# Three of four adjacency blocks transposed by DMA instead of TensorE, with the loads, stores and degree sums around them moved

## The chip, the core and the metric

One core of a Trainium2 chip runs the whole program. The metric is the device time of one execution in microseconds (us), as a median of several runs; lower is better. Engines are named as in the profile: PE is TensorE (PEld its weight loads), DVE is VectorE, ACT is ScalarE, POOL is GpSimd, SP is SyncE. SPq is the queue from which SP issues DMAs.

## The reference

A graph of 2048 nodes with 256 features; `adj` is a 2048x2048 int32 matrix. Two layers, each behind a layer norm and with a residual:

```python
h = relu(layernorm(x))
mask = (adj > 0)
agg = mask @ h / max(mask.sum(1), 1)
x = x + relu(concat(h @ W_self + b_self, agg @ W_nb + b_nb) @ W_comb + b_comb)

state = relu(layernorm(x))
for _ in range(5):
    a_in  = adj   @ (state @ in_W.T  + in_b)
    a_out = adj.T @ (state @ out_W.T + out_b)
    a = concat(a_in, a_out, state)
    r, z = sigmoid(a @ r_W.T + r_b), sigmoid(a @ z_W.T + z_b)
    h_hat = tanh(concat(a_in, a_out, r * state) @ h_W.T + h_b)
    state = (1 - z) * state + z * h_hat
x = x + tanh(state @ o1_W.T + o1_b) @ o2_W.T + o2_b
```

The second layer needs the adjacency both as it is and transposed, and its row sums and column sums (the "degrees", with which the biases in_b and out_b are multiplied).

## The kernel before

The instruction streams are written out by hand for each engine; semaphores alone order them, so each engine works strictly in the order of its own stream. Nodes go in four blocks of 512 (index b, NB = 4), each of four tiles of 128 rows (BT = 4); there are NT = 16 tiles.

**Loading.** The adjacency comes as 32 pieces of 256 rows x 512 columns, 512 KB of int32 each, into a ring of three slots (`ring`, in the tensor WG). SP issues piece k once ACT has converted piece k-3 (L262 to L266). ACT converts each piece in two instructions to fp16 in `A` (function `convert`, L773) with the row sum as a by-product in `degA`; each conversion adds one to the semaphore `conv`.

**The first layer's loop** (L473 on PE, L855 on ACT, L1111 on DVE) has 64 steps i, with b = i // 16 and m = i % 16. For each step PE transposes four 128x128 fp16 blocks of `A` into a PSUM bank (`turn_adj`, L402; it runs LEAD = 3 steps ahead). The even results are copied to `AT` by ACT, the odd ones by DVE (`move_adj`, L785 and L1047), each copy with the column sum as a by-product in `degT`. DVE makes the mask `AT > 0` (`make_mask`, L1055, four buffers in the tensor DR). PE multiplies (`mean_sum`, L418): four matmuls of 512 columns on `hi_lo` (the normed input, split into two fp16 halves) and four of one column that count the mask's ones. After each block there are two calls of `dense` (L441), the weights of the layer, then on DVE the residual, the next layer norm (`residual`, `row_stats`, `variance`, `newton`, `normed`) and the turned state (`turn_h2`). The result x1 goes from SBUF (`xs`) to DRAM (`x1_d`), issued by POOL (L340), and comes back at the end. ACT copies the finished state to `SN` when that store has landed.

**The spread** (L487 on PE). Before any gate, both products of adjacency and state are made for four blocks: `spread(b)` has 16 tiles of 8 matmuls on `AT`, `A` and `SN`. Blocks 0 and 2 write banks 0 to 3, blocks 1 and 3 banks 4 to 7 (`gate_bank`). ACT and DVE empty the banks (`out_pq`). Two calls of `spread_degrees` (L506) inside spread(0) spread the row sums (w = 0) and column sums (w = 1) over all partitions, 16 matmuls each on diagonal matrices that DVE makes (`diag`, L1153); DVE copies the results out of banks 4 to 7 (`out_degrees`, L1158). Meanwhile SP stores twelve quadrants of `AT` and `A`, 1 MB each, to DRAM (`quad_d`, L274), DVE makes sums of quadrants in place (`quad_sums`, L1203, four instructions for each of x = 0, 1) and SP stores these as well.

**The steps** (L721) then alternate groups of gate matmuls (`gate_group`) with products of stored quadrants (`products`), by a seven-multiplication scheme for 2x2 blocks; n counts halves of the node range from FIRST = -2.

Several things share memory. The normed input `h32` lies in AT[:, 1], the weights' sums `scaled` in AT[:, 2], the fused weights `fusedS` in AT[:, 3]; each must have been used up before `AT` is written there.

## Time and profile before

| what | us |
|---|---|
| runs | 1234.11 median of 3 (1233.86 to 1236.0) |
| profiled execution, its own time | 1233.81 |
| its span | 1232.0 |
| first layer's loop on PE, first mask matmul to the last `dense` of block 3's first half | 27.76 to 139.79 |
| spread(0) to spread(3) | 139.79 to 256.41 |
| from the first gate group on | 256.41 to 1232.0 |

The profiled execution is 0.30 us below the median. All times inside it count from the span's start. A matmul's duration in the rows is longer than the distance to the next, since matmuls are pipelined; the cost of a group of them on PE is read from start to start.

### The profile page before, as it was taken

How to read it: one execution, taken by the hardware profiler on the slowest of the kernel's cores; microseconds unless marked ns; L12 is line 12 of the kernel's file. 1: busy time of each engine (PE TensorE's matmuls, PEld its weight loads, DVE VectorE, ACT ScalarE, POOL GpSimd, SP SyncE). 2: the span in 40 equal slices, each digit the busy share in tenths (PEclk: the TensorE clock that was granted, in tenths of full speed). 3: DMA queues.
4: the chain of work that ended last, by engine and by line, in shares of the span. 5: the costliest groups of instructions: out<-in, count | busy, mean ns of one | idle time of the engine just before them, and what ended most of it. 6: DMA issues, size and time to landing. Idle time of an engine off the chain costs nothing.

```text
span 1232.0 us, 12870 instructions
## 1 busy us (share of the span) xinstructions
PE 1221.4 (99%) x4872; PEld 590.6 (48%) x4872; DVE 759.4 (62%) x1276; ACT 285.0 (23%) x556; POOL 15.4 (1%) x15
## 2 busy tenths in 40 slices
PE   8999999999999999999999999999999999999998
PEld 5666654444444444444444444444444444444445
DVE  6677744787985464487357339726825864662674
ACT  5756200022322021033112113301202230120121
POOL 4000000000000000000000000000000000000000
PEclk9999999999999999999999999999999999999999
DMA  9454643960008604800740660192085039015202
GB/s 330 159 166 172 241 186 126 351 248 0 1 34 317 229 1 159 302 18 34 284 160 0 228 250 1 39 357 82 1 299 179 1 132 332 14 66 207 90 1 69
DMA packets 44507, 180.61 MB, mean 147 GB/s; under 512 B 3490, under 2 KB 13475, under 8 KB 29347
## 3 DMA queue, kind: packets, MB, share of 16 engines
q1 hardware_dynamic: 43440, 176.04, 39.5%
q0 software_dynamic: 720, 3.67, 0.8%
q8 instruction: 36, 0.59, 0.2%
q10 hardware_dynamic: 290, 0.14, 0.0%
q14 instruction: 21, 0.16, 0.0%
HBM read 144.71 MB, written 35.13 MB: 146 GB/s over the span
## 4 chain that ended last, share of the span: by engine, by line
PE 86%; DVE 3%; issue 1%; ACT 0%; DVEq 0%
PE bank L347 84%; PE bank L517 1%; DVE LF L1199 0%; DVE GR L1346 0%; DVE first_GZ L1346 0%; DVE first_GH L1319 0%; DVE first_GZ L1349 0%; DVE GR L1349 0%; DVE ST L1322 0%; DVE u_buf L1383 0%; DVE GR L1303 0%; PE bank L467 0%; ACT GR L951 0%; DVE H L1095 0%; DVE AT L1052 0%
## 5 line engine op out<-in xcount | busy, mean ns | idle before, releaser
L347 PE MATMUL bank<-slot,LF 128*128 128x512 f16 x1792 | 389.4, 379 | 0.0
L347 PEld LDWEIGHTS bank<-slot,LF 128*128 128x128 f16 x1792 | 175.3, 98 | 210.1 <-issue 2.3
L347 PE MATMUL bank<-X,W 128*128 128x512 f32 x384 | 180.5, 592 | 0.0
L347 PE MATMUL bank<-XT,W 128*128 128x512 f32 x288 | 135.3, 592 | 0.0
L347 PEld LDWEIGHTS bank<-X,W 128*128 128x128 f32 x384 | 72.5, 190 | 88.0 <-issue 86.9
L347 PE MATMUL bank<-AT,SN 128*128 (+1 forms) x256 | 97.0, 379 | 0.0
L347 PE MATMUL bank<-A,SN 128*128 (+1 forms) x256 | 97.0, 379 | 0.0
L1245 DVE TENSOR_TENSOR u_buf<-bank,m_buf 128x512 f32<-128x512 f32 x16 | 11.1, 691 | 134.0 <-PE bank L347 134.0
L347 PEld LDWEIGHTS bank<-XT,W 128*128 128x128 f32 x288 | 54.7, 190 | 68.9 <-issue 68.2
L767 ACT ACTIVATE m_buf<-bank 128x512 f32<-128x512 f32 x46 | 27.4, 595 | 231.9 <-PE bank L347 231.9
L347 PE MATMUL bank<-DR,work 128*128 128x512 f16 x256 | 67.1, 386 | 1.8 <-DVE DR L1063 1.6
L347 PE MATMUL bank<-XS,W 128*128 128x512 f32 x128 | 65.4, 592 | 0.0
L347 PE MATMUL bank<-ST,W 128*128 128x512 f32 x120 | 61.3, 592 | 0.0
L951 ACT ACTIVATE GR<-GR,col 128x512 f32<-128x512 f32 x40 | 28.8, 720 | 99.7 <-DVE GR L1349 51.7
L347 PE MATMUL bank<-first_X,W 128*128 128x512 f32 x96 | 45.2, 593 | 0.2 <-DVE RT L1283 0.2
L951 ACT ACTIVATE GZ<-GZ,col 128x512 f32<-128x512 f32 x32 | 23.1, 722 | 85.6 <-DVE GZ L1349 55.3
L951 ACT ACTIVATE GH<-GH,col 128x512 f32<-128x512 f32 x32 | 23.1, 722 | 85.5 <-DVE GH L1349 56.4
L347 PE MATMUL bank<-GR,W 128*128 128x512 f32 x80 | 40.9, 592 | 0.0
L767 ACT ACTIVATE A<-WG 128x512 f16<-128x512 int32 x64 | 39.5, 621 | 0.6 <-DMA WG<-in_adj 0.6
L347 PEld LDWEIGHTS bank<-A,SN 128*128 (+1 forms) x256 | 25.1, 98 | 29.9
L347 PEld LDWEIGHTS bank<-AT,SN 128*128 (+1 forms) x256 | 25.1, 98 | 29.7
L347 PEld LDWEIGHTS bank<-XS,W 128*128 128x128 f32 x128 | 24.3, 190 | 30.6 <-issue 30.6
(217 smaller groups left out, 1420.5 us busy)
## 6 DMA issues: line engine op xcount, KB each, us to landing
slot<-quad_d SPq DMA_DIRECT2D x112, 1024.0 KB, 5.1
WG<-in_adj SPq DMA_DIRECT2D x32, 512.0 KB, 4.2
quad_d<-AT SPq DMA_DIRECT2D x12, 1024.0 KB, 5.0
quad_d<-A SPq DMA_DIRECT2D x12, 1024.0 KB, 8.6
quad_d<-spare SPq DMA_DIRECT2D x4, 1024.0 KB, 4.0
SN<-in_x SPq DMA_DIRECT2D x2, 1024.0 KB, 10.4
x_d<-SN POOLq DMA_DIRECT2D x4, 512.0 KB, 3.2
x1o<-x_d SPq DMA_DIRECT2D x1, 2048.0 KB, 8.4
```

What stands on the lines that cost most here:

```text
L347: return pe.matmul(o, l, r, start=start, stop=stop, skip_group_check=again)
L517: last = pe.transpose(o[:, q * P:q * P + P], ST[:, f, n0:n0 + P], ident)
L767: return nc.scalar.activation(o, i, ACT.Copy, scale=scale, **kw)
L951: nc.scalar.activation(buf[:, tile, :], buf[:, tile, :], ACT.Tanh if j == 2 else ACT.Sigmoid, bias=col[:, 10 + 2 * j + f:11 + 2 * j + f]). ...
L1245: v.tensor_tensor(u3, b[:, :], m1, ALU.add).then_inc(prod_dve, 1)
```

## The change

- Blocks 1 to 3 of `AT` are no longer made by PE, ACT and DVE. SP issues for each of the 12 groups j of four tiles (b = 1 + j // 4, c = j % 4) four DMA transposes from `A` to `AT`, each of 128 partitions x 512 fp16 (128 KB, four 128x128 blocks). A group is issued when `conv` has reached 4(j + 5) and, from the fifth on, when group j - 4 has landed. Block 0 stays as it was.
- `make_mask` of blocks 1 to 3 waits, at each fourth step, for the four transposes of its group.
- The row loads from the fourth piece on are issued by POOL instead of SP. The x1 stores are issued by ACT instead of POOL, ahead of the square root of the layer norm. The store of the fused weights goes from POOL to SP, ahead of the transposes.
- ACT's conversions run further ahead: at step i the count reaches 5 + i + max(0, i - 8) // 3 instead of 5 + i.
- The column sums of blocks 1 to 3, 48 instructions (`column_sums`), are made by ACT behind the loop from `AT`, with a throw-away output in `trash`. DVE's reduction of them, the second set of diagonals, `spread_degrees(1)` and `out_degrees(1)` move from spread(0) into spread(2) and its surroundings, and DVE's `out_degrees(1)` goes between `quad_sums(0, 0)` and `quad_sums(0, 1)`.
- `h32` moves from AT[:, 1] to AT[:, 3], `fusedS` from AT[:, 3] to AT[:, 1].

```diff
 LEAD = 3
+TURNS = 4
...
+        trash = [at(f"trash{i}", (202 + i) * KB, [P, BN], FP16)[:, :] for i in range(2)]
+
...
         hi_lo = work[:, :].bitcast(FP16).rearrange("p (t s d) -> p t s d", t=NT, s=2)
-        diag = work[:, 8192:16384].bitcast(FP16).rearrange("p (w t n) -> p w t n", w=2, t=NT)
+        diag = [work[:, 8192:12288].bitcast(FP16).rearrange("p (t n) -> p t n", t=NT),
+                WG[:, :, :].rearrange("p k n -> p (k n)")[:, 0:1024].bitcast(FP16).rearrange("p (t n) -> p t n", t=NT)]
...
         L0 = late[3][:, 4 * D:4 * D + 4 * P].rearrange("p (k r) -> p k r", k=4)
-        h32 = AT[:, 1, :, :].rearrange("p t n -> p (t n)").bitcast(FP32).rearrange("p (t d) -> p t d", t=NT)
+        h32 = AT[:, 3, :, :].rearrange("p t n -> p (t n)").bitcast(FP32).rearrange("p (t d) -> p t d", t=NT)
...
             "p (w j n) -> p w j n", w=2, j=2)
-        fusedS = AT[:, 3, :, :].rearrange("p t n -> p (t n)").bitcast(FP32)[:, 0:4 * GATES].rearrange(
+        fusedS = AT[:, 1, :, :].rearrange("p t n -> p (t n)").bitcast(FP32)[:, 0:4 * GATES].rearrange(
...
         at_act, at_dve = sem("at_act"), sem("at_dve")
+        at_in = [sem(f"at_in{i}") for i in range(TURNS)]
...
             adj_v = adj.rearrange("(b h r p) (c w) -> b c h p r w", b=NB, h=2, r=2, p=P, c=4)
-            for k in range(2 * 4 * NB):
-                b, c, h = k // 8, k // 2 % 4, k % 2
-                if k >= RING:
-                    sp.wait_ge(conv, 2 * (k - RING + 1))
-                sp.dma_start(ring[:, k % RING, :, :], adj_v[b, c, h]).then_inc(ld_ring[k % RING], 16)
+            for k in range(RING):
+                sp.dma_start(ring[:, k, :, :], adj_v[0, k // 2, k % 2]).then_inc(ld_first[k], 16)
+            sp.wait_ge(fused_out, 8)
+            sp.dma_start(fused_d, fusedS).then_inc(st_fused, 16)
+            for j in range(4 * (NB - 1)):
+                b, c = 1 + j // 4, j % 4
+                sp.wait_ge(conv, 4 * (j + 5))
+                if j == 0:
+                    sp.wait_ge(st_fused, 16)
+                if j == 4:
+                    sp.wait_ge(setup_done, 1)
+                if j == 8:
+                    sp.wait_ge(hT_ready, NB)
+                    sp.wait_ge(h_lo, 4)
+                if j >= TURNS:
+                    sp.wait_ge(at_in[j % TURNS], 64 * (j // TURNS))
+                for q in range(BT):
+                    sp.dma_start_transpose(AT[:, b, BT * c:BT * c + BT, q * P:q * P + P],
+                                           A[:, c, BT * b + q, :]).then_inc(at_in[j % TURNS], 16)
...
             sp.wait_ge(conv, 4 * NT)
-            sp.wait_ge(at_act, NT * NB // 2)
-            sp.wait_ge(at_dve, NT * NB // 2)
+            sp.wait_ge(at_act, NT // 2)
+            sp.wait_ge(at_dve, NT // 2)
+            for i in range(TURNS):
+                sp.wait_ge(at_in[i], 64 * (NB - 1))
...
                                         ALU.add).then_inc(gsum, 1)
-            pool.wait_ge(fused_out, 8)
-            pool.dma_start(fused_d, fusedS).then_inc(st_fused, 16)
-            for b in range(NB):
-                pool.wait_ge(x1_ready, BT * (b + 1))
-                pool.dma_start(x1_d[:, BT * b:BT * b + BT, :], xs[:, BT * b:BT * b + BT, :]).then_inc(st_x1, 16)
+            adj_v = adj.rearrange("(b h r p) (c w) -> b c h p r w", b=NB, h=2, r=2, p=P, c=4)
+            for k in range(RING, 2 * 4 * NB):
+                pool.wait_ge(conv, 2 * (k - RING + 1))
+                pool.dma_start(ring[:, k % RING, :, :],
+                               adj_v[k // 8, k // 2 % 4, k % 2]).then_inc(ld_ring[k % RING], 16)
...
                     turn_h2(i // NT - 1)
-                if i + LEAD < NT * NB:
+                if i + LEAD < NT:
...
                     last = mm(gate_bank[t // BT][:, (t % BT) * P:(t % BT) * P + P], one16[:, :],
-                              diag[:, w, t, :], True, True)
+                              diag[w][:, t, :], True, True)
...
             pe.wait_ge(sn_lo, NB - 1)
-            pe.wait_ge(at_act, NT * NB // 2)
-            pe.wait_ge(at_dve, NT * NB // 2)
+            pe.wait_ge(at_act, NT // 2)
+            pe.wait_ge(at_dve, NT // 2)
+            for i in range(TURNS):
+                pe.wait_ge(at_in[i], 64 * (NB - 1))
...
             pe.wait_ge(s_dve, NB)
-            spread_degrees(1)
...
             spread(0, NT - BT, NT).then_inc(agg_done, 1)
+            spread(1, 0, NT).then_inc(agg_done, 1)
+            pe.wait_ge(pq_act, 2)
+            pe.wait_ge(pq_dve, 2)
+            spread(2, 0, 8)
+            pe.wait_ge(pq_act, 4)
+            pe.wait_ge(pq_dve, 4)
+            pe.wait_ge(diag_ready, 2)
+            spread_degrees(1)
+            spread(2, 8, NT).then_inc(agg_done, 1)
             pe.wait_ge(deg_out, 2 * NB)
-            for b in range(1, NB):
-                if b > 1:
-                    pe.wait_ge(pq_act, 2 * (b - 1))
-                    pe.wait_ge(pq_dve, 2 * (b - 1))
-                spread(b, 0, NT).then_inc(agg_done, 1)
+            spread(3, 0, NT).then_inc(agg_done, 1)
...
                 if r == 0:
-                    act.wait_ge(ld_ring[k % RING], 16 * (k // RING + 1))
+                    if k < RING:
+                        act.wait_ge(ld_first[k], 16)
+                    else:
+                        act.wait_ge(ld_ring[k % RING], 16 * (k // RING))
...
                 act.wait_ge(tr_ready, i + 1)
-                if i == NT:
-                    act.wait_ge(hT_ready, NB)
-                    act.wait_ge(h_lo, 4)
-                if i == 3 * NT:
-                    act.wait_ge(st_fused, 16)
...
+
+            def column_sums(b):
+                for m in range(NT):
+                    i = NT * (b - 1) + m
+                    if i >= 2:
+                        act.wait_ge(deg_sum, i - 1)
+                    copy(trash[i % 2], AT[:, b, m, :], accum_out=degT[:, m, b:b + 1]).then_inc(deg_sum, 1)
+
+            def store_x1(b):
+                act.wait_ge(x1_ready, BT * (b + 1))
+                act.dma_start(x1_d[:, BT * b:BT * b + BT, :], xs[:, BT * b:BT * b + BT, :]).then_inc(st_x1, 16)
...
                 def root():
+                    store_x1(b)
...
+            converted = 4
             for i in range(NT * NB):
-                k = 2 * (i // 4 + 1) + i % 4 // 2
...
                     move_adj(0)
-                if k < 8 * NB:
-                    convert(k, i % 2)
+                while converted < min(4 * NT, 5 + i + max(0, i - 8) // 3):
+                    convert(converted // 2, converted % 2)
+                    converted += 1
...
                     block_end(i // NT - 1)[0]()
-                if i % 2 == 0 and i:
+                if i % 2 == 0 and 0 < i < NT:
...
                 stage()
+            for i in range(TURNS):
+                act.wait_ge(at_in[i], 64 * (NB - 1))
...
-            for b in range(NB):
+            column_sums(1)
+            column_sums(2)
+            out_pq(0)
+            column_sums(3)
+            for b in range(1, NB):
...
                 dve.wait_ge(tr_ready, i + 1)
-                if i == 3 * NT + 1:
-                    dve.wait_ge(st_fused, 16)
...
                 b, m = i // NT, i % NT
-                if i % 2 == 0:
+                if i < NT and i % 2 == 0:
                     dve.wait_ge(at_act, i // 2 + 1)
-                else:
+                if i < NT and i % 2 == 1:
                     dve.wait_ge(at_dve, i // 2 + 1)
+                j = (i - NT) // 4
+                if i >= NT and i % 4 == 0:
+                    dve.wait_ge(at_in[j % TURNS], 64 * (j // TURNS + 1))
...
                     sums(i // NT - 1)
-                if i % 2 == 1:
+                if i % 2 == 1 and i < NT:
...
             dve.wait_ge(conv, 4 * NT)
-            dve.wait_ge(at_act, NT * NB // 2)
             v.tensor_reduce(degs[:, 0, :], degA[:, :, :], mybir.AxisListType.X, ALU.add)
-            v.tensor_reduce(degs[:, 1, :], degT[:, :, :], mybir.AxisListType.X, ALU.add)
...
-            for w in range(2):
+            def diagonals(w):
                 for t in range(NT):
-                    ins = v.tensor_scalar(diag[:, w, t, :], id16[:, :], degs[:, w, t:t + 1], None, ALU.mult)
-            ins.then_inc(diag_ready, 1)
+                    ins = v.tensor_scalar(diag[w][:, t, :], id16[:, :], degs[:, w, t:t + 1], None, ALU.mult)
+                ins.then_inc(diag_ready, 1)
+
+            diagonals(0)
...
             turned(NB - 1)
-            dve.wait_ge(h2T_ready, NB)
-            out_degrees(1, degT_all)
-            dve.wait_ge(deg_out, 2 * NB)
...
             out_pq(1)
+            dve.wait_ge(at_act, NT // 2)
+            dve.wait_ge(deg_sum, NT * (NB - 1))
+            link(v.tensor_reduce(degs[:, 1, :], degT[:, :, :], mybir.AxisListType.X, ALU.add))
+            diagonals(1)
             dve.wait_ge(quads_out, 16 * 12)
-            for x in range(2):
-                quad_sums(0, x)
+            quad_sums(0, 0)
+            dve.wait_ge(h2T_ready, NB)
+            out_degrees(1, degT_all)
+            dve.wait_ge(deg_out, 2 * NB)
+            quad_sums(0, 1)
...
             first_change(FIRST)

```

On PE, in the loop of block 1 (steps of `mean_sum`: bank<-DR,work are the mask matmuls, bank<-one,DR the counts, bank<-id,A the transposes). Before, three steps, with the numbers at the rows' starts left out:

```order
L347 MATMUL bank<-DR,work 128x512 [waits mask_ready]
L347 MATMUL bank<-DR,work 128x512 x3
L436 MATMUL bank<-one,DR 128x1 x4
L415 MATMUL bank<-id,A 128x128 [waits at_act,conv]
L415 MATMUL bank<-id,A 128x128 x3
L347 MATMUL bank<-DR,work 128x512 [waits mask_ready]
L347 MATMUL bank<-DR,work 128x512 x3
L436 MATMUL bank<-one,DR 128x1 x4
```

After the change, at the same place:

```order
L370 MATMUL bank<-DR,work 128x512 [waits mask_ready]
L370 MATMUL bank<-DR,work 128x512 x3
L459 MATMUL bank<-one,DR 128x1 x4
L370 MATMUL bank<-DR,work 128x512 [waits mask_ready]
L370 MATMUL bank<-DR,work 128x512 x3
L459 MATMUL bank<-one,DR 128x1 x4
```

The four transposes and their waits have left each step; what is left waits for the mask alone.

On SP, between the loads of the inputs and the quadrant stores. Before (WG<-in_adj are the adjacency's pieces):

```order
L260 DMA A<-in_w_comb 128x4x256
L266 DMA WG<-in_adj 128x2x512 x3
L266 DMA WG<-in_adj 128x2x512 [waits conv] x29
L274 DMA quad_d<-AT 256x1x2048 [waits at_dve,at_act,conv]
```

After the change, the beginning and the end of the same stretch:

```order
L270 DMA WG<-in_adj 128x2x512 x3
L272 DMA fused_d<-AT 128x3072 [waits fused_out]
L286 DMA_TRANSPOSE AT<-A 128x4x128 [waits st_fused,conv]
L286 DMA_TRANSPOSE AT<-A 128x4x128 x3
L286 DMA_TRANSPOSE AT<-A 128x4x128 [waits conv]
L286 DMA_TRANSPOSE AT<-A 128x4x128 x3
...
L286 DMA_TRANSPOSE AT<-A 128x4x128 [waits at_in3,conv]
L286 DMA_TRANSPOSE AT<-A 128x4x128 x3
L297 DMA quad_d<-AT 256x1x2048 [waits at_in1,at_in0,at_in2,at_dve,at_in3,at_act,conv]
```

The 29 waiting loads have gone to POOL, and 48 transposes stand in their place, ahead of the quadrant stores.

On DVE, masks (DR<-AT) around the end of block 1's loop. Before:

```order
L1063 TENSOR_SCALAR DR<-AT 128x512 [waits mask_used,at_dve]
L1063 TENSOR_SCALAR DR<-AT 128x512 [waits mask_used,at_act]
L1052 TENSOR_SCALAR AT,degT<-bank 128x512 [waits tr_ready]
L1063 TENSOR_SCALAR DR<-AT 128x512 [waits mask_used,at_dve]
L1104 SCALAR_TENSOR_TENSOR SN<-H,SN 128x4x256 [waits sn_hi]
```

After the change:

```order
L1110 TENSOR_SCALAR DR<-AT 128x512 [waits mask_used]
L1110 TENSOR_SCALAR DR<-AT 128x512 [waits mask_used,at_in3]
L1110 TENSOR_SCALAR DR<-AT 128x512 [waits mask_used]
L1151 SCALAR_TENSOR_TENSOR SN<-H,SN 128x4x256 [waits sn_hi]
```

The copies out of PSUM (AT,degT<-bank) are gone, and one mask in four waits for a transpose group.

## Rows read from the trace of the kernel before

**Rows 1.** The page's chain of work that ended last, shares by engine.

```profile
PE 86%; DVE 3%; issue 1%; ACT 0%; DVEq 0%
```

**Rows 2.** PE's and PEld's waits, 27.7 to 136.3 us: total us, times, longest.

```profile
PE bank L347 <- DVE DR L1063: 1.6, 6, 0.3
...
PEld bank L347 <- DVE DR L1063: 3.5, 10, 0.5
...
PEld bank L415 <- ACT A L767: 0.4, 2, 0.2
```

**Rows 3.** PE's timeline, three places of the loop: start us, us, instruction, count.

```profile
84.14 1.03 PE L347 MATMUL bank<-DR,work 128*128 128x512 f16 x4
...
85.11 0.38 PE L415 MATMUL bank<-id,A 128*128 128x128 f16 x4
85.33 1.03 PE L347 MATMUL bank<-DR,work 128*128 128x512 f16 x4
...
131.26 1.03 PE L347 MATMUL bank<-DR,work 128*128 128x512 f16 x4
...
134.32 1.02 PE L347 MATMUL bank<-DR,work 128*128 128x512 f16 x4
...
135.29 1.02 PE L347 MATMUL bank<-DR,work 128*128 128x512 f16 x4
```

**Rows 4.** Groups by form, 27.7 to 136.3 us: busy us, mean ns | idle before.

```profile
L1052 DVE TENSOR_SCALAR_CACHE_REDUCE AT<-bank 128x512 f16<-128x512 f16 x31 | 21.2, 685 | 4.9 <-PE bank L415 4.4
```

**Rows 5.** DMA issues of the page: KB each, median us from issue to landing.

```profile
WG<-in_adj SPq DMA_DIRECT2D x32, 512.0 KB, 4.2
...
W<-fused_d SPq DMA_DIRECT2D x12, 128.0 KB, 4.0
```

**Rows 6.** Stretches: busy us (instructions) of each engine, PEclk, DMA share, GB/s.

```profile
80.00:108.00 28.00, 27.31 (x233) 18.27 (x231) 21.61 (x68) 17.36 (x52) 0.53 (x1) 1.00 0.49 167
...
210.00:215.00 5.00, 5.00 (x25) 2.27 (x24) 4.96 (x3) 0.00 (x0) 0.00 (x0) 1.00 1.02 403
```

**Rows 7.** Line 289, SP's issue of 128 KB loads: ns min/median/max.

```profile
L289 SPq DMA_DIRECT2D W<-fused_d x12: 457/574/1352, 221.4 to 232.4; - x12
```

**Rows 8.** ACT's timeline: 20th conversion, two in a row, last copy before the spread's.

```profile
47.47 0.62 ACT L767 ACTIVATE A<-WG 128x512 f16<-128x512 int32 x1
...
59.01 0.62 ACT L767 ACTIVATE A<-WG 128x512 f16<-128x512 int32 x1
59.53 0.19 ACT L767 ACTIVATION_READ_ACCUMULATOR A<-WG 128x1 f32 x1
59.62 0.62 ACT L767 ACTIVATE A<-WG 128x512 f16<-128x512 int32 x1
...
162.47 0.60 ACT L767 ACTIVATE ST<-bank 128x512 f32<-128x512 f32 x1 [1.90 <-PE bank L467]
```

**Rows 9.** DVE's timeline around the degrees and the quadrant sums.

```profile
151.16 5.29 DVE L1153 TENSOR_SCALAR work<-id,degs 128x128 f16<-128x128 f16 x32
...
164.49 2.48 DVE L1161 CAST H<-bank 128x512 f16<-128x512 f32 x4 [0.88 <-PE bank L347]
...
201.35 1.29 DVE L1174 COPY first_X<-bank 128x512 f32<-128x512 f32 x2 [26.27 <-PE bank L347]
202.56 2.28 DVE L1209 TENSOR_TENSOR AT<-AT 128x4096 f16<-128x4096 f16 x1
...
220.66 1.22 DVE L1218 TENSOR_TENSOR first_X<-first_X,first_X 128x1024 f32<-128x1024 f32 x1
228.98 1.29 DVE L1174 COPY first_X<-bank 128x512 f32<-128x512 f32 x2 [7.10 <-PE bank L347]
...
257.40 0.68 DVE L1278 TENSOR_TENSOR first_XS<-ST 128x512 f32<-128x512 f32 x1
```

**Rows 10.** PE's timeline at the first gate group.

```profile
256.41 1.88 PE L347 MATMUL bank<-first_X,W 128*128 128x512 f32 x4
...
258.98 1.88 PE L347 MATMUL bank<-first_X,W 128*128 128x512 f32 x4
```

More of the change, by code:

```diff
@@ L182, in graph_net @@
         at_act, at_dve = sem("at_act"), sem("at_dve")
+        at_in = [sem(f"at_in{i}") for i in range(TURNS)]
+        deg_sum = sem("deg_sum")
+        ld_first = [sem(f"ld_first{i}") for i in range(RING)]
         mask_ready, mask_used = sem("mask_ready"), sem("mask_used")
```

## Prediction, made before the changed kernel ran

> **What bounds the kernel now.** I read the chain of waits first: it runs through PE for 86% of the span [rows 1], so what shortens PE's stream shortens the program, as long as nothing else becomes later than PE. Then the waits of PE in the first layer's loop, the only stage that the change touches heavily: PE and its weight loads together stand still for 1.6 + 3.5 = 5.1 us of 108.6 us there (the two are partly the same gaps), and the one named is DVE's mask [rows 2]. So the loop is PE's own work with some small gaps that DVE causes. Last, the timeline of PE for the cost of one step: with transposes the mask matmuls of two steps start 85.33 - 84.14 = 1.19 us apart; the last steps, which have none, 135.29 - 134.32 = 0.97 us [rows 3].
>
> **What PE sheds.** A step's four transposes cost 1.19 - 0.97 = 0.22 us of PE. 48 of the 64 steps' transposes go: 48 x 0.22 = 10.6 us. This is on the path, whole, since PE is the path.
>
> **What DVE and ACT shed.** DVE copies every second transposed tile: 0.685 us each [rows 4], 24 of them in blocks 1 to 3, or 16.4 us, between its masks. Where DVE has a burst (the residual and the norm of the block before) these copies make a mask late; that is what the 3.5 us of weight-load waits on the mask are. With 16.4 us less to do in three blocks, most of these go, but not those that sit behind a chain of small dependent instructions. Bounds: 0 and 3.5 us. I take 2.2, nearer the upper end because the copy was the largest thing between two masks. ACT loses 24 copies too, but PE hardly waited for it (0.4 us, and for its conversions at that [rows 2]), so that is worth nothing.
>
> **What DMA takes over, and its unknown price.** 48 transposes of 128 KB, from SBUF to SBUF. The trace shows no such transfer, so I write t for the time by which one follows another, and ask from which t the masks become late. The first group can go once 20 conversions are done. In the trace that is at 47.47 + 0.62 = 48.1 us [rows 8], and after the change about there or a little before. The last group is wanted by the mask of step 60. Its matmuls start at 131.26 us now [rows 3]; the 47 transposes ahead of them leave, 10.4 us, and the 2.2 us of gaps, which makes 118.7. Let the last group land 3 us after its issue (a 128 KB load lands in 4.0 us [rows 5], part of it queueing). Then the transposes are hidden while 48.1 + 48t + 3 < 118.7, so t < **1.41 us**. Ends for t: the bytes alone, at the 403 GB/s that the stores reach [rows 6], take 0.33 us, and an issue of a 128 KB transfer takes SP 0.46 us at least, 0.57 us in the middle [rows 7]; at the other end, if the transfers do not overlap at all and each takes what such a load takes to land, 4.0 us [rows 5]. I take a t under 1.4, because all the other transfers of the trace, the small ones too, are issued 0.4 to 0.6 us apart and overlap, so 0.6 is the nearer row, with a factor of two to spare. The long end stays as a rival.
>
> The Trainium skill speaks on both sides here, and no run of this case shows it. Its page "Advanced Engine Details and Errata", section "X-Bar Transpose (TRN2)", says that transposing DMAs are as fast as regular ones, 350 to 400 GB/s; by that a transfer is an estimated 0.35 us and all 48 are hidden. Its page "VectorE: DVE Perf Modes", section "The three transpose paths", gives 1309 ns for one 128x128 block by DMA; taken as a rate, four blocks would be an estimated 5.2 us and the program some 180 us slower. The same table gives 390 ns for TensorE, where our trace has four in 0.22 us, so that I read the table as the latency of one alone.
>
> **DMA room.** In the loop the engines are busy to 0.49 at 167 GB/s [rows 6]. The transposes add 6.3 MB in about 75 us, 84 GB/s, at the same efficiency another 0.25. Even at half the efficiency it is 0.98, just room. The row loads move from SP to POOL; a piece is converted in two times 0.61 us (59.01 to 59.62 [rows 8]) and landed in 4.2 us [rows 5], so three slots give a piece every (4.2 + 1.2) / 3 = 1.8 us, while PE's loop of 112.0 us (the table), less 12, takes 100 / 32 = 3.1 us for one. A POOL-issued load may land 3 us later and still cost nothing.
>
> **Behind the loop.** ACT gets 48 column sums. They start behind its copy at 162.47 and, at 0.61 us each like conversions, take 29.3 us, with one out_pq (1.1 us) between: done at about 194, relative to the old times. DVE wants them after its copies of 201.35 [rows 9], so 7 us of cover. DVE now makes there 16 diagonals (5.29 / 2 = 2.6 us), a reduction (0.2) and out_degrees(1) (2.5) [rows 9], 5.3 us more between 202.6 and its next wait. It used to wait 7.1 us there before the copies of 228.98 [rows 9], so this fits with 1.8 us to spare. But PE makes these degrees only after half of spread(2), at about 215, and DVE reaches the copies at 202.6 + 2.8 + 9.1 = 214.5: within 1 us. quad_sums(0, 1) then ends at 227, its last 1 MB store some 4 us later, and first_sums, which waits for that store, may start up to 1 us late. DVE's first own sum used to start at 257.40 and be ready at 258.1, PE wants it at 258.98 [rows 9, 10]: 0.9 us of cover. I book 0.4 us. PE's spread_degrees(1) costs the same at its new place. The store of x1 by ACT delays a small square root that has several steps of cover: nothing.
>
> **The sum.** 10.6 + 2.2 - 0.4 = 12.4 us, less 0.5 for the first groups of block 1, whose conversions come only just ahead: 11.9 us. From the profiled execution, 1233.81 - 11.9 = 1221.9; the median lies 0.3 above it, so **1222.2 us**. Its own range: all gaps of rows 2 gone gives 1218, none gone and 2 us lost behind the loop gives 1227.
>
> **Rival 1, slower: the transposes set the pace.** The place is between conversion and mask of blocks 1 to 3: SP issues in order, groups wait for the fourth before them, and PE, whose steps need the mask, stands. Each us of t above 1.41 costs 48 us. It decides against the change from t = 1.41 + 11.9 / 48 = **1.66 us**. At the middle of my two ends, t = 2.2, the program takes 1222.2 + 48 x 0.79 = 1260; at 4.0 us it takes 1222.2 + 48 x 2.59 = 1346. For it: a transfer that reorders 2-byte elements is unlike any in the trace, and a break-even at four times the plain copy's 0.4 is not far. Against: nothing else here is issued so slowly. The twelve quadrant stores behind the transposes take 12 MB / 403 GB/s = 31 us and are wanted by DVE 63 us after the loop (202.56 against 139.79), so they have cover whatever t is.
>
> **Rival 2: faster, but partly paid back.** t between 1.41 and 1.6, or the degrees late behind the loop. If a column sum took 0.62 + 0.19 = 0.81 us (its accumulator's read not overlapped [rows 8]), the sums would end at 203, 0.4 us late and within DVE's slack; at 0.9 us they end at 207, DVE starts 4.8 us late with 1.8 us of slack, and the end moves by 3 us. That gives 1225, and with t in that stretch up to 1231.
>
> **Rival 3: PE is relieved, but DVE's gaps stay or grow**, since a mask that waits for a group holds up everything behind it on DVE, the residual included. PE's 10.6 us remain, the rest not: 1223 to 1226, inside the forecast's range.
>
> **Chances.** Forecast with rival 3 (1217 to 1228): 0.54. Rival 2 beyond it (1228 to 1231.6): 0.05. Rival 1 0.41, of which 0.06 falls within 0.2% of before (t between 1.6 and 1.71) and 0.35 above. A difference of 0.2%, 2.5 us, is about what a measurement of this kernel can tell from none. Faster 0.59, same 0.06, slower 0.35. The range must reach into rival 1: from 1217, with 0.03 below, up to t = 2.3, 1222.2 + 43 = 1265, with 0.17 above.
>
> **What would show it.** In the profile of the changed kernel: mask matmuls of blocks 1 to 3 starting 0.97 us apart; no row of PE or DVE waiting for DMA AT<-A over 1 us; the transposes' issues on SPq under 1.4 us apart; the loop's end near 127.5 instead of 139.79; the first gate group near 244.5 instead of 256.41, with no wait of PE for first_XS. Rival 1 shows as DVE masks that wait for DMA AT<-A four by four, and SPq busy back to back. Rival 2 shows as PE waiting in spread(2) or at spread(3)'s start. The prediction is wrong if one DMA transpose costs more than 1.4 us of the queue.

## The result and the profile after

The changed kernel took **1254.35 us** (median of 4 runs, 1250.63 to 1259.96) against 1233.98 (median of 4, 1232.43 to 1236.0). The ratio is 1.0168, its 95% interval 1.012 to 1.0216: slower by 1.7%, where 1222.2 us was forecast. The profiled execution is the fastest of the four: 1250.63 us, with a span of 1248.8 us; before it was 1232.0. What the rows below add up is this difference of 16.8 us.

The chain of work that ended last was PE for 86% [rows 1]. In the page of the changed kernel DVE and DMA have taken a part of it:

```profile
PE 84%; DVE 7%; DMA 5%; SPq 1%; issue 1%; ACT 1%; DVEq 0%
```

The waits of the first layer's loop, changed kernel, 27 to 160 us (total us, times, longest), which answer to [rows 2]:

```profile
ACT A L796 <- DMA WG<-in_adj: 41.7, 22, 5.2
PEld bank L370 <- DVE DR L1110: 22.6, 10, 7.0
PE bank L370 <- DVE DR L1110: 21.0, 7, 6.9
DVE DR L1110 <- DMA AT<-A: 18.2, 5, 7.8
...
DVE SN L1151 <- ACT SN L796: 11.5, 3, 8.9
```

PE waits 21.0 us for masks where it waited 1.6. The masks wait for two things: for the transposed blocks (18.2 us), and for ACT's copy of the state (11.5). The first line stands behind the second of these: ACT's conversions wait 41.7 us for row loads.

PE's timeline, changed kernel (start us, us, instruction, count, idle before), which answers to [rows 3]:

```profile
60.16 1.89 PE L370 MATMUL bank<-DR,work 128*128 128x512 f16 x4 [4.41 <-DVE DR L1110]
...
81.68 1.89 PE L370 MATMUL bank<-DR,work 128*128 128x512 f16 x4 [6.65 <-DVE DR L1110]
83.51 1.87 PE L370 MATMUL bank<-DR,work 128*128 128x512 f16 x4
85.32 1.76 PE L370 MATMUL bank<-DR,work 128*128 128x512 f16 x4
...
123.53 1.89 PE L370 MATMUL bank<-DR,work 128*128 128x512 f16 x4 [6.93 <-DVE DR L1110]
...
136.49 1.03 PE L370 MATMUL bank<-DR,work 128*128 128x512 f16 x4
137.45 1.02 PE L370 MATMUL bank<-DR,work 128*128 128x512 f16 x4
...
151.58 1.97 PE L370 MATMUL bank<-WG,ST 128*128 128x256 f32 x8
```

Where nothing waits, steps are 0.97 us apart (136.49, 137.45), as forecast. But three stalls of 4.4 to 6.9 us stand in the loop, and behind each some steps start 1.8 us apart (81.68, 83.51, 85.32). The windows show why: where PE had just stood still, the granted clock of the next stretch is low. Windows of the changed kernel (stretch, its length, busy us and instructions of PE, PEld, DVE, ACT, POOL, then PEclk, DMA share, GB/s), which answer to [rows 6]:

```profile
60.00:70.00 10.00, 8.86 (x48) 5.40 (x48) 6.14 (x16) 2.67 (x8) 1.78 (x3) 0.85 1.20 189
70.00:80.00 10.00, 4.18 (x32) 2.11 (x32) 2.97 (x13) 3.03 (x10) 1.45 (x2) 1.00 1.17 203
80.00:90.00 10.00, 8.32 (x49) 4.08 (x50) 5.66 (x18) 4.80 (x13) 2.17 (x3) 0.66 1.21 232
90.00:100.00 10.00, 9.35 (x61) 6.08 (x59) 5.57 (x15) 4.96 (x14) 2.17 (x3) 1.00 1.29 238
...
120.00:130.00 10.00, 6.47 (x28) 3.91 (x29) 3.66 (x9) 4.42 (x11) 0.00 (x0) 0.66 0.84 155
```

A mean of 0.66 is part of the stretch at the lower of the two levels (1.2 GHz) and the rest at 2.4. The column beside it is the cause looked for below: from 60 to 100 us the 16 DMA engines are busy to 1.17 to 1.29 (over 1, since the shares of the queues are added and their packets overlap in the records), and yet move only 189 to 238 GB/s. Before, 0.49 of them moved 167 [rows 6].

**The balance of the loop.** The last `dense` of block 3's first half starts at 151.58; before, it started at 136.25. So the loop lost 15.3 us. Gained: 10.6 us of transposes and 1.6 us of old waits. Lost: 21.0 us of waits on masks, and at the low clock (1 - PEclk) times PE's busy time, 1.3 + 2.8 + 2.2 us in three of the windows above and 0.1 in one not shown, 6.4 us. Together 21.0 + 6.4 - 10.6 - 1.6 = 15.2. That closes.

**Where the stalls come from.** The chain of the changed kernel in order of time (start us, us, what):

```profile
59.91 2.67 SPq L286
62.62 3.54 SPq L286
66.20 1.52 SPq L286
67.76 13.54 DMA AT<-A
81.33 0.30 DVE DR L1110
81.68 1.89 PE bank L370 x4
...
109.68 10.03 DMA WG<-in_adj
...
120.27 0.80 ACT A L796 x3
121.07 0.95 ACT SN L796
...
123.53 1.89 PE bank L370 x4
```

There are two kinds. At 81.68 the mask waited for a transposed group that was issued at intervals of up to 3.5 us and then took 13.5 us to land. At 123.53 it waited for ACT's copy of the state, which stands in ACT's order behind a conversion made ahead of need, whose row load took 10.0 us to land. So neither the queue of SP nor the transposes alone: the row loads are late as well. The page's DMA issues (KB each, median us to landing), and the trace on line 286 and the landings of the transfers of the tile AT (six of the 54 are stores), both of the changed kernel, which answer to [rows 5, 7]:

```profile
WG<-in_adj POOLq DMA_DIRECT2D x29, 512.0 KB, 7.5
```

```profile
L286 SPq DMA_TRANSPOSE AT<-A x48: 1188/1297/4768, 46.8 to 132.3; - x48
...
DMA to landing us min/median/max: 2.5/8.1/16.3
```

A load lands in 7.5 us instead of 4.2. A transpose occupies SP's queue for 1.30 us at the median and up to 4.77; on average one follows another after (132.3 - 46.8) / 47 = 1.82 us. Of these 85.5 us SP spent some 5.7 waiting for ACT's conversions, so a transpose itself costs the queue 1.70 us on average.

**Behind the loop** little happened. From 151.58 to the second group on `first_X` PE gained nothing and lost this (waits of PE, changed kernel, 160 to 290 us):

```profile
PE bank L370 <- DVE first_XS L1322: 1.2, 1, 1.2
```

### The profile page after: what moved, and what is told of

It is laid out like the page before. It is cut to its first block, busy times and chain, and to the rows that moved or that the text cites. A ratio compares the mean times of both kernels' runs of the same rounds, so it can differ in the third digit from the quotient of the medians.

```text
span 1248.8 us, 12468 instructions
## 1 busy us (share of the span) xinstructions
PE 1216.9 (97%) x4680; PEld 582.1 (47%) x4680; DVE 745.6 (60%) x1228; ACT 300.0 (24%) x604; POOL 34.0 (3%) x39
## 4 chain that ended last, share of the span: by engine, by line
PE 84%; DVE 7%; DMA 5%; SPq 1%; issue 1%; ACT 1%; DVEq 0%
PE bank L370 83%; DMA WG<-in_adj 2%; SPq L286 1%; DMA AT<-A 1%; PE bank L540 1%; DMA SN<-in_x 1%; ACT A L796 1%; DMA quad_d<-A 0%; DVE W L1484 0%; DVE spare L1255 0%; DVE A L1258 0%; DVE spare L1253 0%; DVE LF L1243 0%; PE bank L490 0%; DVE stat L1036 0%
## 5 line engine op out<-in xcount | busy, mean ns | idle before, releaser
L370 PE MATMUL bank<-DR,work 128*128 128x512 f16 x256 | 70.8, 409 | 21.4 <-DVE DR L1110 21.0
L1289 DVE TENSOR_TENSOR u_buf<-bank,m_buf 128x512 f32<-128x512 f32 x16 | 11.1, 692 | 134.0 <-PE bank L370 134.0
L796 ACT ACTIVATE A<-WG 128x512 f16<-128x512 int32 x64 | 39.7, 622 | 41.7 <-DMA WG<-in_adj 41.7
L993 ACT ACTIVATE GH<-GH,col 128x512 f32<-128x512 f32 x32 | 23.1, 722 | 85.5 <-DVE GH L1393 56.4
L370 PEld LDWEIGHTS bank<-DR,work 128*128 128x128 f16 x256 | 22.3, 102 | 41.5 <-DVE DR L1110 22.6
## 6 DMA issues: line engine op xcount, KB each, us to landing
SN<-in_x SPq DMA_DIRECT2D x2, 1024.0 KB, 10.4
```

Of the source, the lines that this page charges most:

```text
L370: return pe.matmul(o, l, r, start=start, stop=stop, skip_group_check=again)
L796: return nc.scalar.activation(o, i, ACT.Copy, scale=scale, **kw)
L993: nc.scalar.activation(buf[:, tile, :], buf[:, tile, :], ACT.Tanh if j == 2 else ACT.Sigmoid, bias=col[:, 10 + 2 * j + f:11 + 2 * j + f]). ...
L1289: v.tensor_tensor(u3, b[:, :], m1, ALU.add).then_inc(prod_dve, 1)
```

## The experiments

Theory A: transposes and row loads want the 16 DMA engines together for more time than the loop has; either alone would fit. Rivals: B, the transposes by SP's queue are too slow by themselves; C, POOL is a bad issuer of the row loads; D, the moves around the transposes (the run-ahead conversions, degrees and column sums behind the loop) cost the time; E, the stall comes from ACT's order. Each ratio below is to the kernel before, with a 95% interval.

**1. The moves without the transposes by DMA.** All four blocks are transposed by TensorE, with everything else of the change. The constant DB (blocks that TensorE transposes) replaces the fixed 1 of the change in this and some later kernels; the core of the edit:

```diff
+DB = 4
-            for j in range(4 * (NB - 1)):
+            for j in range(4 * (DB - 1), 4 * (NB - 1)):
...
-                if i + LEAD < NT:
+                if i + LEAD < NT * DB:
...
-                if i < NT and i % 2 == 1:
+                if i < NT * DB and i % 2 == 1:
```

> The change without its DMA transposes: row loads issued by POOL, x1 stores by ACT, the fused store by SP, h32 and the degree work at their new places, but all four blocks transposed by TensorE and copied by ACT and DVE as before. Theory (the transposes fill the DMA engines and make the row loads late): without them nothing is late, 1233 to 1236 us, and a row load lands in 4 to 5 us. Rival (loads issued by POOL are slow by themselves): loads land in 7 to 8 us here too, ACT waits for them by 20 us or more, and the time is 1240 or above.

Measured: 1239.06 us, ratio 1.0042 (1.0025 to 1.0059), 3 us above what the theory expected. So D is worth 5 us, not the 20. The DMA transposes, in place of TensorE's, add another 15.3 on top of it, although PE sheds 10.6. The loads, issued by POOL here too, land in a median of 4.4 us: POOL as issuer is not what delays them.

**2. Plain copies in place of the transposes**, same bytes, same order, in runs of 256 bytes. AT then doesn't hold the transposed adjacency.

```diff
-                    sp.dma_start_transpose(AT[:, b, BT * c:BT * c + BT, q * P:q * P + P],
-                                           A[:, c, BT * b + q, :]).then_inc(at_in[j % TURNS], 16)
+                    sp.dma_start(AT[:, b, BT * c:BT * c + BT, q * P:q * P + P],
+                                 A[:, c, BT * b + q, :].rearrange("p (k n) -> p k n", k=BT)).then_inc(at_in[j % TURNS], 16)
```

> The changed kernel with each of the 48 DMA transposes replaced by a plain copy of the same 128 KB with the same 256-byte runs and the same waits (the transposition of blocks 1 to 3 is left out, so their numbers are another matrix's). Theory (it is the transposing that takes DMA engine time, about 1.1 us of all 16 engines per 128 KB): copies cost 0.4 us each, the masks are in time, 1222 to 1226 us. Rival (any SBUF to SBUF transfer in 256-byte runs costs as much): 1245 to 1255 us. Rival (SP's issue of 1.3 us each): visible as issues of under 0.7 us here.

Measured: 1234.6 us, ratio 0.9999 (0.9989 to 1.0009), between the two expectations. A copy occupies SP's queue for 0.65 us (median), half as long as a transpose, and the time is only 4.5 us under experiment 1, of the 10.6 that PE sheds: PE waits 9.0 us for masks, ACT 23.7 us for row loads. So even a copy that is cheap to issue costs something beside the loads. But the other 20 us of the change's 1254 hang on these transfers being transposes. The queues' rows of this kernel, 50 to 110 us, row loads, then copies:

```profile
q0 software_dynamic: 2851, 10.37, 52.3%
q1 hardware_dynamic: 22725, 5.64, 46.0%
```

**3 and 4. Fewer blocks by DMA**: only block 3 (DB = 3, 16 transposes), or blocks 2 and 3 (DB = 2, 32).

```diff
+DB = 3
```

> Only the last block is transposed by DMA (16 transposes), blocks 0 to 2 by TensorE. Theory (DMA engine time): 16 x 1.1 = 18 us of engine time more in a loop whose engines had some 50 us free, but much of it must lie while the last loads still run. PE saves 16 x 0.22 = 3.5 us and loses one wait of up to 3 us: 1230 to 1235. If waits grow linearly with the number of transposes from zero, a third of the full change's loss: 1240.

```diff
+DB = 2
```

> The last two blocks by DMA (32 transposes). Theory: 36 us of engine time more, loads 4.5 to 6 us to landing; PE saves 7 us and waits for masks 8 to 12 us: 1234 to 1240. If only the first group's lateness mattered (block 1 has the shortest lead), this would be near the forecast, 1226 to 1229.

Measured: 1241.51 (ratio 1.006, 1.0043 to 1.0077) and 1240.96 (1.0068, 1.0042 to 1.0094), the first as the rival with linear growth said, the second just above what the theory expected. Over the 1239.06 of no transposes, 16 cost 2.5 us and 32 cost 1.9, neither clearly more than nothing (the intervals overlap); the third 16 cost 13.4 more. It isn't a price for each transpose. PE sheds 3.5 us with every block, and PE's waits for masks are 3.1, 6.0, 13.6 and 21.0 us with 0, 16, 32 and 48: the second and the third block add 7.6 and 7.4, twice what PE sheds. With 16 no mask waits for a transpose at all; the 11.4 us that DVE's masks wait there are for ACT, and the longest of ACT's own waits is 4.8 us for a row load.

**5. The price of one, in a quiet stretch.** The kernel before, with 1 + 8 transposes and then 8 plain copies of the same shape between spread(0)'s stores and spread(2), into a free buffer.

```diff
+            sp.wait_ge(quads_out, 16 * 12)
+            sp.dma_start_transpose(XT16[8], A[:, 0, 0, :]).then_inc(probe[0], 16)
+            sp.wait_ge(probe[0], 16)
+            for i in range(8):
+                sp.dma_start_transpose(XT16[i], A[:, 0, i, :]).then_inc(probe[1], 16)
+            sp.wait_ge(probe[1], 16 * 8)
+            for i in range(8):
+                sp.dma_start(XT16[i], A[:, 0, i, :].rearrange("p (k n) -> p k n", k=BT)).then_inc(probe[2], 16)
```

> The kernel before with a probe on SP in the stretch in which no DMA runs (about 170 to 203 us): one 128 KB transpose alone, then 8 back to back, then 8 plain copies of the same shape. Nothing that PE waits for is touched. Theory: a transpose alone lands in 2.5 to 3 us; 8 follow one another at 1.1 to 1.3 us and the DMA share is near 1 while they run, copies at 0.4 to 0.6 us. Rival (SP's issue is the limit, the engines are not full): 1.3 us each, but a DMA share well under 1.

Its trace, line of the eight transposes, then line of the eight copies (ns min/median/max), each with its landings, and the stretch of the transposes (last three: PEclk, DMA share, GB/s):

```profile
L282 SPq DMA_TRANSPOSE WG<-A x8: 1189/1267/1726, 170.7 to 180.2; - x8
...
DMA to landing us min/median/max: 2.5/2.5/3.5
```

```profile
L285 SPq DMA_DIRECT2D WG<-A x8: 507/602/602, 182.7 to 187.1; - x8
...
DMA to landing us min/median/max: 2.0/2.1/2.1
```

```profile
171.00:181.00 10.00, 10.00 (x48) 4.57 (x47) 1.29 (x2) 1.08 (x2) 0.00 (x0) 1.00 0.54 93
```

Alone, a transpose of 128x512 fp16 occupies SP's queue for 1.27 us, under the 1.41 that the prediction named as its limit, and lands 2.5 us after its issue. The DMA share is 0.54 while they run, where the theory expected one near 1: alone, transposes are limited by their issue on SP, and the 16 engines are half free, as the rival said. The copies go into a free buffer whose rows are 1 KB long, so they are to be compared with experiment 12 and not with experiment 2. The program took 1232.4 us in its one run.

**6. The row loads issued by ACT.**

```diff
-            for k in range(RING, 2 * 4 * NB):
-                pool.wait_ge(conv, 2 * (k - RING + 1))
-                pool.dma_start(ring[:, k % RING, :, :],
-                               adj_v[k // 8, k // 2 % 4, k % 2]).then_inc(ld_ring[k % RING], 16)
...
+                n = k + RING
+                if r == 1 and n < 2 * 4 * NB:
+                    act.wait_ge(conv, 2 * (k + 1))
+                    act.dma_start(ring[:, n % RING, :, :],
+                                  adj_v[n // 8, n // 2 % 4, n % 2]).then_inc(ld_ring[n % RING], 16)
```

> The changed kernel, but the row loads from the fourth on are issued by ACT's hardware queue right after the conversion that frees their slot, not by POOL. Theory (engines full, whoever issues): the same within 5 us of the changed kernel, 1248 to 1256, loads still 7 us or more to landing. Rival (POOL's queue loses against SP's transposes): loads land in 5 us, 1225 to 1238.

Measured: 1252.12 us, ratio 1.0132 (1.0101 to 1.0163), loads landing in 7.4 us. Rival C falls. The Trainium skill says why one should expect that (page "DMA: Bandwidth & Descriptors", section "Issuing engines are not separate DMA queues"): all issuers' DMAs run on the same 16 engines and interleave. The run agrees, 1252 against 1254 us, with no difference beyond the intervals.

**7. The transposes without the row loads of blocks 1 to 3.** All 48 transposes stay, and so does all work of PE, DVE and ACT.

```diff
-            for k in range(RING, 2 * 4 * NB):
+            for k in range(RING, 8):
...
-                    else:
+                    elif k < 8:
```

> The changed kernel without the row loads of blocks 1 to 3 (24 of 32 pieces are left out; ACT converts what lies in the ring, so blocks 1 to 3 hold block 0's numbers). All 48 DMA transposes and all waits on them stay. Theory (transposes and row loads together overfill the DMA engines, and each makes the other late): alone, a transpose follows the other in 1.3 us and lands in 2.5 to 4 us, masks come in time, 1222 to 1227 us. Rival (SP's issue of 1.3 us each, 48 in 62 us at best, is the limit by itself): 1235 or more.

Measured: 1224.14 us, ratio 0.9907 (0.9884 to 0.993), close to the 1222.2 that was forecast for the change itself. Its trace, line 286 with its landings, and PE's timeline at the loop's end:

```profile
L286 SPq DMA_TRANSPOSE AT<-A x48: 1191/1267/2212, 48.6 to 115.5; - x48
...
DMA to landing us min/median/max: 2.4/2.5/17.8
```

```profile
126.41 1.97 PE L370 MATMUL bank<-WG,ST 128*128 128x256 f32 x8
```

The transposes are back at the quiet 1.27 and 2.5 us, the loop ends 9.8 us before the old 136.25, and PE waits 1.5 us for masks. B falls as a cause on its own: the same transposes by the same queue are fast enough as soon as the loads are away. (Without loads the conversions can't be late either, so this kernel takes away two things at once: the loads' share of the engines, and their lateness.)

The DMA queues' rows put the shares side by side (packets, MB, share of 16 engines). Changed kernel, 50 to 130 us: transposes, then row loads.

```profile
q1 hardware_dynamic: 23802, 5.74, 59.5%
q0 software_dynamic: 2855, 10.38, 49.6%
```

Kernel before, 50 to 120 us: row loads.

```profile
q1 hardware_dynamic: 5358, 10.32, 44.4%
```

Without the late loads, 50 to 115 us: transposes.

```profile
q1 hardware_dynamic: 24948, 6.02, 50.1%
```

Share times stretch gives the time of all 16 engines: the loads took 0.444 x 70 = 31.1 us before and 39.7 (0.496 x 80) now; the transposes 32.6 us alone (0.501 x 65, for 6.02 MB, which is 46 of 128 KiB, so 0.71 us each) and 47.6 (0.595 x 80, for 44, so 1.09 each) beside the loads. At the prices of each alone, 31 + 33 + 3 for the x1 store make 67 us, for a stretch that was forecast to last some 60 us (70 less 10). So even then no room was left.

But that is the smaller part. Plain copies take nearly as much: in experiment 2 the loads took 0.523 x 60 = 31.4 us, the copies 27.6 (0.460 x 60, 0.64 each) and the store 2.6, together 61.6 of 60 us, and that kernel is 20 us faster than the changed one. There the loads kept the price that they have alone. Beside transposes they didn't: loads and transposes together took 87 us instead of 64. So theory A holds in a stronger form: together, both kinds of transfer take up the engines longer than each does alone, and this sets the changed kernel apart from experiment 2 more than the sum of their own prices does.

**8. Experiment 1 with the old order of conversions**, for the 5 us of rival D.

```diff
-                while converted < min(4 * NT, 5 + i + max(0, i - 8) // 3):
+                while converted < min(4 * NT, 5 + i):
```

> The kernel without DMA transposes but with the moved issues and degree work, now also with the old order of ACT's conversions (one a step, no running ahead). Theory (of the 5 us that the moves cost, some 3 us come from conversions that stand ahead of ACT's PSUM copies and wait for a load): 1235 to 1236.5, the rest being DVE's later start on the gates' sums, 1.2 us. Rival (POOL's issue of the loads costs it): 1238 or more.

Measured: 1235.69 us, ratio 1.001 (0.9999 to 1.0021). So 3.4 of the 5 us come from converting ahead of need, and the rest is within what can be told from nothing; PE's wait of 1.2 us for `first_XS` is still there.

**9. Experiment 3 with an even lead.**

```diff
+DB = 3
-                while converted < min(4 * NT, 5 + i + max(0, i - 8) // 3):
+                while converted < min(4 * NT, 5 + i + i // 4):
```

> Only the last block by DMA, as in the kernel with 16 transposes, but ACT's conversions gain their lead evenly from the first step on (one more in four steps). Theory (ACT's waits for loads in the run-ahead are what the small version loses): 1234 to 1238 instead of 1241.5. If the 16 transposes themselves are late by DMA contention: no better, 1240 to 1243.

Measured: 1239.17 us, ratio 1.0034 (1.0023 to 1.0046): 2.3 better than experiment 3 (the intervals just overlap), and still not faster than before. ACT once more stands 4.8 us before a run-ahead conversion, and DVE 5.0 us for the state copy behind it.

**10 and 11. The state copy ahead of the conversions.** ACT puts no further conversions ahead in steps 9 to 14 of a block, in the changed kernel and in experiment 3.

```diff
-                while converted < min(4 * NT, 5 + i + max(0, i - 8) // 3):
+                s = i - max(0, i % NT - 8) if NT <= i and i % NT < 15 else i
+                while converted < min(4 * NT, 5 + s + max(0, s - 8) // 3):
```

> The changed kernel with one difference in ACT's order: in steps 9 to 14 of each block after the first no further conversion is put ahead, so that the copy of the finished state (SN) stands ahead of the conversions of which the last waited 5.2 us for its load. Theory (the 6.9 us stall of PE in block 2 comes from that order, the others from masks that wait for transposes): 1243 to 1248 us instead of 1254, and no wait of DVE for ACT's SN over 2 us. Rival (the stall only moves to the masks, as the conversions behind come later): 1250 or more.

```diff
+DB = 3
-                while converted < min(4 * NT, 5 + i + max(0, i - 8) // 3):
+                s = i - max(0, i % NT - 8) if NT <= i and i % NT < 15 else i
+                while converted < min(4 * NT, 5 + s + max(0, s - 8) // 3):
```

> The same order of ACT in the kernel with 16 transposes. Theory: the one stall of 3.4 us goes, PE sheds 3.5 us of transposes, the moved degree work costs 1.2 to 1.9: 1234 to 1237. A version faster than before would show here if anywhere: the sum is before - 3.5 + 1.9 - some gaps of DVE, so 1232 to 1236.

Both missed. Measured: 1257.7 us (ratio 1.0185, 1.0168 to 1.0202) and 1249.53 (1.014, 1.0123 to 1.0157). The waits of experiment 10's loop, 27 to 160 us (its profiled execution is the slowest of five, 1264.3 us):

```profile
ACT A L796 <- DMA WG<-in_adj: 37.2, 19, 3.5
DVE DR L1111 <- DMA AT<-A: 28.2, 4, 9.7
...
ACT SN L796 <- DMA x_d<-SN: 16.5, 2, 11.4
...
PE bank L370 <- DVE DR L1111: 15.8, 7, 7.5
PE bank L370 <- ACT H L796: 15.8, 2, 9.2
```

The copy of the state now waits for the landing of the x1 store, up to 11.4 us, with the conversions behind it; PE's wait for masks fell from 21.0 to 15.8, and 15.8 of waits for ACT's copy `H` came in its place.

Experiment 11 shows what the second wait is. From its trace, ACT, then PE (start us, us, instruction):

```profile
76.81 0.62 ACT L797 ACTIVATE A<-WG 128x512 f16<-128x512 int32 x1
...
87.35 0.58 ACT L797 ACTIVATE H<-bank 128x512 f32<-128x512 f32 x1
```

```profile
87.98 3.58 PE L371 MATMUL bank<-WG,H 128*128 128x256 f32 x8 [5.24 <-ACT H L797]
```

The conversions held back in steps 9 to 14 all come after them, 11 in a row, and the copy `H`, for which PE waits, stands behind them and behind the loads that they want. No DMA transpose has been issued by then (the first is at 95.9 us). In experiment 11 PE's waits for masks fell from the 6.0 us of experiment 3 to 2.1, as was meant, and 11.3 us of waits for `H` came instead. So these two kernels don't settle E: the order of ACT's stream does decide part of the stalls, but the edit that removed one brought in another of its own. What speaks against E as the cause of the whole loss is experiment 7: ACT's order is that of the changed kernel, and without late loads it stalls nothing.

**12. Copies in rows of 1 KB** instead of 256 bytes (like experiment 2, AT doesn't hold the transposed adjacency).

```diff
-                    sp.dma_start_transpose(AT[:, b, BT * c:BT * c + BT, q * P:q * P + P],
-                                           A[:, c, BT * b + q, :]).then_inc(at_in[j % TURNS], 16)
+                    sp.dma_start(AT[:, b, BT * c + q, :], A[:, c, BT * b + q, :]).then_inc(at_in[j % TURNS], 16)
```

> The changed kernel with each of the 48 transposes replaced by a plain copy of the same 128 KB in rows of 1 KB instead of 256 bytes (the transposition of blocks 1 to 3 is left out). With 256-byte rows it was 1234.6. Theory A (the number of short packets fills the engines): loads land in 5 us and the time is 1224 to 1228. Theory B (the bytes and the longer chain load, convert, DMA, mask do it): 1232 to 1236 as with the short rows.

Measured: 1231.16 us, ratio 0.9982 (0.9964 to 0.9999). Its queues' rows, 50 to 108 us, copies and row loads:

```profile
q0 software_dynamic: 2891, 10.52, 55.1%
q1 hardware_dynamic: 6295, 5.74, 28.8%
```

That is neither of the two expectations, a little under the second. The copies take 0.288 x 58 = 16.7 us of the engines, where transposes took 47.6 and copies in 256-byte runs 27.6; the times are 1231, 1254 and 1235. The 3.4 us between the two kinds of copy are hardly more than the intervals leave open. Of the 11.9 us of forecast gain 2.8 by the medians are there and 9.1 are not: 5.0 of these are rival D's (experiment 1). The other 4 were not taken apart; the loads land in 5.8 us even here, with the engines busy to 0.89, and the way from load over conversion and DMA to mask is longer than before. It is not a solution, as it doesn't transpose.

## Why the prediction was wrong

- **What bounds the kernel, what PE sheds:** right. The steps are 0.97 us apart. With the loads away 9.8 of 12.3 us arrive at the loop's end; that loop also began 1.2 us later (28.99 against 27.76), so it is 11.1 us shorter.
- **The pace of the transposes, t < 1.41 us:** the value taken was right for a transpose alone (1.27 us, landing in 2.5, where 3 were assumed), and it did not decide. In the mix t was 1.82 and the landing 8.1. The condition 48.1 + 48t + 3 < 118.7 used prices of a quiet queue for a queue that the change itself makes full. It also let SP issue without a pause, although each group waits for four more conversions: with the loads away SP still took (115.5 - 48.6) / 47 = 1.42 us for one, some 6.6 of the 66.9 us waiting for ACT. So there was no "factor of two to spare" even there. The last sentence of the prediction, wrong if a transpose costs over 1.4 us of the queue, catches the mean of the mix (1.70) and misses its median (1.30).
- **"DMA room" is the step that failed.** It put the transposes at 0.25 of the engines, from the efficiency of the loads, which is 0.131 MB / (167 / 0.49 GB/s) = 0.38 us each. Alone they take 0.71, beside the loads 1.09. The text had the half efficiency as its worst case, called 0.98 "just room" and charged it nothing. Nor did it allow that the new transfers make the loads dearer: these took 39.7 us of the engines instead of 31.1. It should have been a rival with a price: with the shares adding up to 1.13 loads landed in 8.7 us instead of 4.2. Its other sentence carried the means to see that: three slots give a piece every (landing + 1.2) / 3 us, and PE takes one every 3.1. With the 8.7 us that the loads of 50 to 130 us took to land that is 3.3 us. The 3 us of allowed delay (4.2 to 7.2) were used up and more, and this is where ACT's 41.7 us of waiting come from.
- **What DVE and ACT shed** (2.2 us of gaps): not borne out. With the loads away the waits on masks are 1.5 us of PE and 2.3 of its weight loads, where they were 1.6 and 3.5, and the loop is 11.1 us shorter, 0.5 more than the transposes alone. In the changed kernel much longer gaps took their place.
- **Behind the loop:** booked at 0.4 us, measured 1.2. The column sums were covered, as forecast. DVE's first own sum is what PE waits for; the 0.9 us of cover were not enough.
- **Not seen at all:** that converting ahead of need costs (3.4 us, experiments 1 and 8), since it puts ACT's copies behind loads that are not wanted yet (ACT waits 7.7 us for loads in experiment 1, 3.6 in experiment 8); and that each stall is followed by steps at the low clock, 6.4 us in sum, 0.3 of the stalls again.
- **Rival 1** (groups late, PE stands, slower) is what the profile shows, at 0.35 for slower. Its price by t = 1.82 would be 1222.2 + 48 x 0.41 = 1242; it missed the second kind of stall and the clock. The measured time is inside the range because Rival 1 had been given room up to t = 2.3, for a transpose that is slow by itself; that it covers transposes slowed by the loads is luck.

**What stays open.** Why a transpose takes 1.09 us of the engines beside loads and 0.71 alone isn't settled. Packets of two queues on one engine overlap in the records (the shares sum to 1.13), so part of it may be one queue's packet waiting for the other's. Copies show no such growth: one in 1 KB rows takes 0.38 us of the engines beside loads (16.7 us for 5.74 MB) and 0.39 alone (experiment 5, 0.521 of the 6 us from 183 to 189, for eight). The Trainium skill (page "DMA: Bandwidth & Descriptors", section "Queues, rings and completion order") says that each engine takes turns between queues, packet by packet; that would give such an overlap, but no run here separates waiting from work. Rival E was not tested by an order of ACT that moves the state's copy ahead without bunching the conversions. Nor was it tried to bring the loads earlier, with a longer ring, or to move the transposes behind the loop.

## What to carry to other kernels

Before work is moved from a busy engine to "idle" DMA, add up the engine time of all transfers of that stretch, each at its own price and over the new, shorter length of the stretch; a sum near 1 is a rival with a price, not room, and a sum of prices taken alone can be too low, as here, where beside each other both kinds of transfer cost more. If a ring of few slots feeds the stage, compute the landing time at which it becomes the pace, and ask what stands in order behind its consumer. A copy of the same bytes in place of the new transfer, and the new transfer without its neighbours, are two cheap kernels that tell a slow transfer from a full channel.

## What the runs showed of the hardware

- A DMA transpose of 128x512 fp16 from SBUF to SBUF occupies SP's queue for 1.27 us where a copy of 128 KB takes 0.60 (experiment 5). One after another they move at most 103 GB/s (0.131 MB in 1.27 us), with the 16 engines busy to 0.54. The Trainium skill calls such transposes as fast as regular DMAs, 350 to 400 GB/s (page "Advanced Engine Details and Errata", section "X-Bar Transpose (TRN2)"); at this size that isn't so here. Nor is the 1309 ns of its page "VectorE: DVE Perf Modes" (section "The three transpose paths") for one 128x128 block a rate: four blocks took 1.27 us.
- Beside the row loads, transposes left the engines slower than copies of the same bytes did: 215 GB/s in the changed kernel from 50 to 130 us at a share of 1.13, against 285 with plain copies in 256-byte runs (50 to 110 us, 1.03) and 299 with 1 KB rows (50 to 108 us, 0.89).
- The same 10.4 MB of row loads took up the 16 engines for 31.1 us alone, 31.4 beside 256-byte copies and 39.7 beside transposes.
- After its three long stalls (4.41, 6.65 and 6.93 us) PE's steps stood 1.8 us apart instead of 0.97, with a granted clock of 0.85, 0.66 and 0.66 in the windows that hold them. So a late mask cost three to four tenths more than the profile's wait shows (1.3, 2.8 and 2.2 us).
